# Graph kernel on one core: the score passes' look-ups wait for four different steps instead of one

## The reference

```
h = (x @ Wg).reshape(n, HEADS, HID)
a_s = jnp.einsum('nhc,hc->nh', h, att_s)
a_d = jnp.einsum('nhc,hc->nh', h, att_d)
logits = jax.nn.leaky_relu(a_s[src] + a_d[dst] + ew[:, None], NEG_SLOPE)
```

## Time and profile before

| | us |
|---|---|
| median of 3 runs | 5898.77 |
| lowest, highest | 5892.44, 5901.37 |
| the profiled execution | 5945.03 |
| its span | 5943.2 |
| first score pass, first look-up to last `difference` | 1363.9 to 1845.7 |
| second | 2267.8 to 2669.7 |
| third | 3088.5 to 3567.6 |

### The profile page before, as it was taken

How to read it: one execution, slowest core, us unless ns; L and a number is a source line. 1 busy time by engine, 2 the same in 40 slices (tenths; PEclk the granted TensorE clock), 3 DMA queues, 4 the chain that set the end, 5 groups by cost and what they waited for, 6 DMA issues and landing times. The chain is left out here.

```text
span 5943.2 us, 108677 instructions
## 1 busy us (share of the span) xinstructions
PE 4271.4 (72%) x24342; PEld 3042.8 (51%) x24342; DVE 3890.1 (65%) x14954; ACT 3291.7 (55%) x11014; POOL 2792.4 (47%) x2718
## 2 busy tenths in 40 slices
PE   3999995556885996665978885976767676864444
PEld 2667663324663555663546662435555565653333
DVE  5999995445777886777867777983456564433223
ACT  1899994334664775664756675873356563112222
POOL 3888884443431224431224331126556565655565
PEclk9999997778997998887989997998988888986666
DMA  2566664666884776774758874754445454432222
GB/s 66 175 194 196 197 191 168 220 225 217 274 272 155 233 239 208 255 254 146 241 194 271 271 262 153 226 179 121 125 155 166 150 166 130 128 118 67 69 76 62
DMA packets 612939, 1072.27 MB, mean 180 GB/s; under 512 B 107736, under 2 KB 128362, under 8 KB 612764
## 3 DMA queue, kind: packets, MB, share of 16 engines
q1 hardware_dynamic: 537308, 944.74, 47.5%
q0 software_dynamic: 75456, 125.65, 8.7%
HBM read 607.70 MB, written 466.24 MB: 181 GB/s over the span
## 5 line engine op out<-in xcount | busy, mean ns | idle before, releaser
L2385 POOL DMA_INDIRECT got_c<-table,src_row x980 | 927.9, 947 | 622.1 <-issue 254.6
L1387 POOL DMA_INDIRECT src_got_s<-table,src_row x588 | 554.6, 943 | 799.6 <-DVE delta_s L1628 595.6
L1971 POOL TENSOR_TENSOR part_m<-part_m,half_sum_m 128x512 f32<-128x512 f32 x147 | 220.7, 1501 | 916.9 <-DVE half_sum_m L2187 916.9
L1980 PE MATMUL bank<-w_all,dt_m 128*128 128x512 f32 x1176 | 567.9, 599 | 36.3 <-DMA dt_m<-delta_t 34.7
L2509 ACT COPY agg_c<-bank 128x512 f32<-128x512 f32 x245 | 143.4, 585 | 661.9 <-issue 214.0
L1542 ACT ACTIVATE z_s<-z_s,shift_s,dev_s 128x128 f32<-128x128 f32 x1176 | 483.5, 486 | 1.4 <-DVE shift_s L1661 0.9
L2435 PEld LDWEIGHTS bank<-w_c,agg_c 128*128 128x128 f32 x1960 | 327.9, 217 | 262.0 <-issue 261.9
L2435 PE MATMUL bank<-w_c,agg_c 128*128 128x128 f32 x1960 | 357.2, 301 | 99.5 <-issue 97.6
L2433 PE MATMUL bank<-bias_c,first_row 128*128 128x512 f32 x490 | 315.9, 731 | 138.1 <-ACT agg_c L2509 113.5
L790 PEld LDWEIGHTS bank<-w_mean,ht 128*128 128x128 f32 x2352 | 313.3, 194 | 143.6 <-issue 143.6
L2410 PE MATMUL bank<-pick_c,got_c 128*128 128x128 f32 x1960 | 317.1, 314 | 71.2 <-DMA got_c<-table,src_row 59.0
(11 more groups left out here) (326 smaller groups left out, 12028.7 us busy)
## 6 DMA issues: line engine op xcount, KB each, us to landing
table<-rows SPq DMA_DIRECT2D x294, 256.0 KB
x_s<-table SPq DMA_DIRECT2D x294, 256.0 KB
x_c<-table SPq DMA_DIRECT2D x245, 256.0 KB
table<-mid_s SPq DMA_DIRECT2D x196, 256.0 KB
table<-z_s SPq DMA_DIRECT2D x196, 256.0 KB
table<-z_c SPq DMA_DIRECT2D x196, 256.0 KB
own_rows_s<-table SPq DMA_DIRECT2D x147, 256.0 KB
pick_t_s<-picks_t SPq DMA_DIRECT2D x147, 256.0 KB
```

Source lines behind the costliest of these rows:

```text
L1387: nc.gpsimd.indirect_dma_start(out=src_got[r][:, g, :], out_offset=None, in_=tables[l].rows, in_offset=bass.IndirectOffsetOnAxis(ap=src_ro ...
L1971: nc.gpsimd.tensor_tensor(flat(part[r]), flat(part[r]), flat(half_sum[r]), ALU.add).then_inc(parts_added, 1)
L1980: nc.tensor.matmul(b_h[k % n_h][:, :], dt[b.slot][:, k, :], w_all[:, l, :, :].rearrange("p h d -> p (h d)"), start=True, stop=True).then_i ...
L2385: nc.gpsimd.indirect_dma_start(out=got[r][:, g, :], out_offset=None, in_=t_in.rows, in_offset=bass.IndirectOffsetOnAxis(ap=src_row[:, t:t ...
```

## The change

Only the wait ahead of the look-ups changes. The first look-up of batch b waits as before. The second, third and fourth each get a wait of their own, for a step of TensorE: in the first and third pass `turn_rows(b-3,1)`, `hidden(b-3,0)` and `product(b-3,0)`; in the second pass `product(b-3,0)`, `turn_rows(b-2,0)` and `product(b-3,1)`.

```diff
                     def _(pool):
+                        def pace(b, g):
+                            if g == 0:
+                                pool.wait_ge(delta_made, b - 3)
+                            elif first:
+                                if g == 1:
+                                    pool.wait_ge(turned, 2 * b - 4)
+                                elif g == 2:
+                                    pool.wait_ge(h_made, 2 * b - 5)
+                                else:
+                                    pool.wait_ge(y_made, 2 * b - 5)
+                            elif g == 1:
+                                pool.wait_ge(y_made, 2 * b - 5)
+                            elif g == 2:
+                                pool.wait_ge(turned, 2 * b - 3)
+                            else:
+                                pool.wait_ge(y_made, 2 * b - 4)
...
                         for b in range(nb):
                             r = b % 4
-                            if b > 3:
-                                pool.wait_ge(delta_made, b - 3)
                             for g in range(GB):
                                 t = b * GB + g
+                                if b > 3:
+                                    pace(b, g)
                                 nc.gpsimd.indirect_dma_start(
```

## The result

| | before | after |
|---|---|---|
| median, us | 5898.58 | 5724.49 |
| lowest, highest, us | 5892.44, 5901.37 | 5706.49, 5734.38 |
| the profiled execution, us | 5945.03 | 5706.49 |

The ratio of the medians is 0.9703, with a 95% interval of 0.9677 to 0.9728: 174 us less. So in what follows differences between single stages of the two profiles add up to more than 174.

The account below looks back on a forecast made before the run. Rows of look-ups delaying TensorE's news were taken to bound the first and third pass. Gains of 68 and 70 us there and 0 in the second, 138 together, took the median from 5899 to 5761 us, range 5695 to 5855.

Parts of the forecast that it names:

- The cause: First pass: look-ups in a row delay news of TensorE's finished work until 1.1 to 1.3 us after the last one's end.
- Rows 2's 8.0 us for the transfers: First and third pass: transfers, 0.84 of 9.52 us, need 8.0 us a turn; gains of 68 and 70 us.
- bound of 180: First and third pass: with turns of 7.54 us, 45 x 4.0 = 180 us off, giving 5719 us.
- The second pass at 0: Second pass: new waits met on arrival, look-ups stay in one row, gain 0; bounds 15 us either way.
- The waits themselves at 0: GpSimd, three passes: three added waits a batch, at most 0.9 us a batch within its idle time, cost nothing.
- The spacing: First and third pass: look-ups 1.6 us apart or more, some 1.5 us to the next turn's first; second pass still 1.25.
- Rival A: First and third pass: transfers at 272 GB/s limit the turn, spread or not; no change, 5899 us; 7%.
- Rival B: First and third pass: single look-ups hold news or transfers near their limit; turn 9.0 us, gain 48, about 5850; 13%.
- Rival C: First and third pass: each spaced look-up delays news separately; with H = 2.8 us, turns of 10.2 us, about 5960; 6%.
- The forecast that the prediction drew from it: All three passes: DMA never contends with a compute engine, so spacing look-ups brings 0 instead of 138 us.

## Why the prediction was right, and where it was off

5761 us was predicted, in a range of 5695 to 5855; 5724 was measured. Step by step:

- **The cause.** Right. TensorE's updates came some 1.0 to 1.4 us after the end of a row's last look-up, and spacing the look-ups freed them. Moving the row moved the delay (ratio 1.0103), gaps without waits removed it (0.9658), and leaving the look-ups out gained as much as spacing them (0.9708).
- **Rows 2's 8.0 us for the transfers.** This is the mis-sized term. I took busy share times turn as a floor, 0.84 x 9.52, although I had noted that part of it is queueing. Measured: 345 GB/s at a share of 1.00, a turn of 7.47 us, just what the last three turns of the earlier trace rows had said. With the measured middle turns in the same sum, 45 x (9.52 - 7.47) + 45 x (9.55 - 7.53) = 183 us in place of 138. 174 were measured. The prediction had this sum as its bound of 180, and set it aside for the 8.0. A small slip beside it: of GpSimd's 582 instructions in `node_chain` 392 are look-ups, not 386.
- **The second pass at 0.** Right: 3 us. All three waits were met on arrival and the look-ups stayed 1.25 us apart. But I stopped at "stays as it is" and did not price what lay there: 52 to 56 us, which the two kernels with gaps in that pass took.
- **The waits themselves at 0.** Right: GpSimd waits 131 us for TensorE in 300, and VectorE's `difference`, which needs the looked-up rows, sat idle for 0.2 us in that time.
- **The spacing.** The sign was 1.6 us or more between look-ups. Within a batch it was met (middle values of the first pass 1.8, 2.0 and 2.3 us), but the first look-up of a batch followed the last of the one before at 1.32 us, where the working had 1.5. It cost nothing that shows: a pair at such a distance is not a row.
- **Rival A, the transfers are the limit.** Fell in the comparison: 272 GB/s became 345. **Rival B, a turn of 9.0 us:** fell. **Rival C, single look-ups hold for H = 2.6 us or more:** fell, since news came through 1.75 us after a look-up's start; the late updates of the changed kernel's first pass came 1.3 to 1.8 us after it. That the kernel with the row after `hidden` met its price, 5960 us and 10.2 us a turn, is chance: there it is the row that holds.
- **The Trainium skill,** page "SBUF — State Buffer", section "Who interferes with whom", says that a DMA never contends with a compute engine. The section is about the SBUF's ports, and against that the runs show nothing: `hidden` takes 1.02 us and `relu` 0.69 us with rows and without. The forecast that the prediction drew from it, that spacing brings nothing, failed on the chips of the comparison: with the same instructions and other gaps the time goes from 0.9612 to 1.0103 of before. On the other chips it held (0.9993 to 1.0005).
- **Not foreseen: that it depends on the chip.** Nothing in the profile of before could tell it. The change itself ran on one chip without the delay and is worth 0.9998 there; on another such chip four kernels that place or leave out the look-ups otherwise gave 0.9993 to 1.0005. The prediction was right for the chips on which the delay exists; compared on one of the others, it would have been wrong, and 5899 us, rival A's "no change", right in its ratio.

What stays open: why the chips differ, and what exactly is held. In both kinds of chip the look-up takes 0.94 us on GpSimd with 0.30 us between. The profile models the ends of TensorE's instructions, so whether the update of a finished instruction is held back, or its last step, isn't told apart either. Whether the delay comes from the writing of the descriptors or from the rows that they move wasn't told apart, since every kernel here looks up rows of one size. That look-ups in rows also lengthen the convolve stages is argued from the stage lengths on the two kinds of chip; no convolve stage was edited.

## What to carry to other kernels

When two engines that wait for different instructions resume at the same moment, look for what had just ended on a third, and don't trust the releaser printed. Where a profile shows this beside rows of indirect transfers on GpSimd, spread those that aren't needed soon, by a wait that is not yet met when it is reached or, where none offers itself, by a small memset. In this kernel 1.55 us from start to start was enough for most turns, and pairs were free when 1.8 us lay between the last of one and the first of the next; another size of transfer may need another gap. Measure on more than one chip before calling such a gain general, and don't take the busy share of the transfers at a slow pace for the time that they need at a fast one.

## What the runs showed of the hardware

- On some chips, four look-ups 1.25 us apart hold the updates of TensorE's semaphores until about 1.0 to 1.4 us after the last one's end; 195 of 357 recorded ones were over 0.3 us late, and of VectorE's and ScalarE's about 1%. At 1.44 us apart 42 of 48 turns still take over 8.5 us; at 1.55 us 4 do, though 66 of 278 updates are over 1 us late. Pairs at 1.25 us were free in the first pass with 1.84 us or more to the next pair, and held with 1.75 us or less.
- On other chips nothing is held. The same program takes 5135 us there and 5895 here, 15% more, with `node_chain` and the granted clock in it the same.
- Transfers of 256 KB and the look-ups together ran at 345 to 352 GB/s at a share of 1.00, without slowing the engines: TensorE was busy for 98 to 99% in that time, and the turn was 7.47 us, against 7.44 with no look-ups at 318 GB/s.
